# Causal attention stage: rows of maxima sent from ScalarE's queue, q and k loaded in six pairs over a group

## The reference

```
x = x + attn_a(layernorm(x))   # causal softmax attention, 16 heads of 16
x = x + ffn(layernorm(x))      # FP4 quantised SwiGLU, 256 -> 704 -> 256
x = x + attn_b(layernorm(x))   # rotary, local window of 128 and every 64th key
x = x + ffn(layernorm(x))
```

```
scores = einsum('bhqd,bhkd->bhqk', Q, K) / sqrt(16)
attn = softmax(scores + causal)      # causal: -inf above the diagonal
O = einsum('bhqk,bhkd->bhqd', attn, V)
```

## Time and profile before

| | us |
|---|---|
| median of 3 runs | 3343.1 |
| lowest, highest | 3340.86, 3345.84 |
| the profiled execution's own time | 3338.47 |
| its span in the trace | 3336.7 |
| span of the attention stage's matmuls, first turn to last turn | 292.3 to 1062.8 |

### The profile page before, as it was taken

One profiled execution on the slowest core, in us unless ns is written; L12 is line 12 of the kernel. 1 busy time (PEld: TensorE's weight loads), 2 busy tenths in 40 slices (PEclk: granted clock), 3 DMA queues, 4 the chain that ended last, 5 costly groups with the idle time before them and its releaser, 6 DMA issues. The chain is left out here.

```text
span 3336.7 us, 92235 instructions
## 1 busy us (share of the span) xinstructions
PE 3098.7 (93%) x34732; PEld 2145.9 (64%) x34828; DVE 2606.8 (78%) x5407; ACT 1746.1 (52%) x3395; POOL 1092.9 (33%) x1631
## 2 busy tenths in 40 slices
PE   3997999999999799999979969999999969999999
PEld 2654777777776477777755535565555537777776
DVE  6547999999997699999959955655655649999997
ACT  3653887788788333333326635555555533333333
POOL 2542121121122222222216654454454432222222
PEclk8996999999999899999989979999999979999999
DMA  3764434434432222222226664445445322222221
GB/s 112 229 218 99 106 90 103 103 90 107 99 89 66 84 85 86 85 86 85 82 70 205 198 161 112 103 110 115 102 108 112 82 72 81 85 85 86 87 87 51
DMA packets 390672, 351.79 MB, mean 105 GB/s; under 512 B 111814, under 2 KB 331846, under 8 KB 390214
## 3 DMA queue, kind: packets, MB, share of 16 engines
q1 hardware_dynamic: 390342, 347.10, 38.6%
HBM read 210.12 MB, written 135.27 MB: 104 GB/s over the span
## 5 line engine op out<-in xcount | busy, mean ns | idle before, releaser
L852 DVE TENSOR_REDUCE aA_nmax<-bank 128x1 f32<-128x512 f32 (+3 forms) x1216 | 714.6, 653 | 69.9 <-PE bank L911 63.6
L895 ACT ACTIVATE aA_prob<-bank 128x512 f32<-128x512 f32 (+1 forms) x1216 | 616.8, 581 | 208.1 <-PE bank L911 202.9
L911 PE MATMUL bank<-aA_ks,aA_qs 96*32 96x512 bf16 (+13 forms) x6144 | 513.0, 321 | 27.0 <-POOL aA_vq L829 24.2
L1279 DVE TENSOR_REDUCE aB_nmax<-bank 128x2 f32<-128x512 f32 (+1 forms) x512 | 324.0, 657 | 212.9 <-remote 120.4
L911 PE MATMUL bank<-aA_qs,aA_ks 99*32 99x512 bf16 (+11 forms) x6144 | 470.2, 314 | 3.5 <-ACT aA_prob L895 1.8
L836 POOL TENSOR_SCALAR_AFFINE_SELECT aA_prob<-aA_prob 128x512 f32<-128x512 f32 x256 | 160.9, 634 | 663.6 <-ACT aA_prob L895 663.6
L911 PE MATMUL bank<-aA_prob,aA_vq 128*32 128x512 f32 (+3 forms) x3072 | 355.9, 490 | 1.4 <-POOL aA_prob L836 0.9
L1342 ACT ACTIVATE aB_prob<-bank 128x512 f32<-128x512 f32 (+1 forms) x512 | 278.2, 572 | 107.9 <-PE bank L1373 103.5
L911 PEld LDWEIGHTS bank<-aA_ks,aA_qs 96*32 96x32 bf16 x6144 | 247.2, 96 | 131.7 <-DVE aA_nmax L852 44.6
L1373 PE MATMUL bank<-aB_ks,aB_qs 96*128 96x256 bf16 (+3 forms) x2048 | 244.7, 258 | 38.8 <-DMA aB_own<-own_d 28.6
L911 PEld LDWEIGHTS bank<-aA_qs,aA_ks 99*32 99x32 bf16 x6144 | 224.8, 96 | 57.1 <-ACT aA_prob L895 19.3
(11 more groups left out here) (240 smaller groups left out, 6497.4 us busy)
## 6 DMA issues: line engine op xcount, KB each, us to landing
parts_A<-pA_part SPq DMA_DIRECT2D x96, 256.0 KB, 3.3
aA_qs<-parts_A SPq DMA_DIRECT2D x192, 128.0 KB, 3.9
aA_ks<-parts_A SPq DMA_DIRECT2D x192, 128.0 KB, 4.0
parts_B<-pB_part SPq DMA_DIRECT2D x96, 256.0 KB, 2.6
aB_qs<-parts_B SPq DMA_DIRECT2D x192, 128.0 KB, 3.9
aB_ks<-parts_B SPq DMA_DIRECT2D x192, 128.0 KB, 4.0
o_A<-aA_o_sb SPq DMA_DIRECT2D x32, 512.0 KB, 3.0
o_B<-aB_o_sb SPq DMA_DIRECT2D x32, 512.0 KB, 3.1
```

Source lines behind the costliest of these rows:

```text
L852: nc.vector.tensor_reduce(dst, src, AX.X, ALU.max, negate=True).then_inc(s["m_taken"], 1)
L895: nc.scalar.activation(dst, src, ACT.Exp, scale=SCALE).then_inc(s["e_taken"], 1)
L911: return nc.tensor.matmul(out, lhsT, rhs, start=start, stop=True, skip_group_check=True)
L1279: nc.vector.tensor_reduce(dst, src, AX.X, ALU.max, negate=True).then_inc(s["max_taken"], 1)
```

## The change

Three things change, in the first attention stage alone.

1. The three DMAs of the maxima's rows leave SyncE's list and enter ScalarE's (`send_rows`), behind the same wait on `rows_ready`. Their place is set by the planner, where they are a piece "rows" on "act" with a cost of 500 ns and a due time of -0.2; a pseudo-engine "dma" adds 3500 ns until they have landed.
2. SyncE waits before each of the six pairs of loads of q and k: pair r of group n+4 waits for pv unit r of group n+1. Before, all six waited once, for the last pv of group n. The load of v for group n+2 moves ahead of them. The first loads of group 3 no longer stand behind the rows of group 0.
3. The planner gets the new costs (5000 ns for q and k in place of 12000, with the new condition), and its order for TensorE, VectorE and ScalarE comes out different.

```diff
-        put("sp qk", "qk", 0, 12000, -2, ("pe", "pv", n - RING, N_PV - 1))
+        put("sp qk", "qk", 0, 5000, -2, ("pe", "pv", n - RING + 1, N_PV // 2))
...
-        put("sp rows", "rows", 0, 3500, 0, ("dve", "turn", n, 0))
+        put("act", "rows", 0, 500, -0.2, ("dve", "turn", n, 0))
+        put("dma", "land", 0, 3500, 0, ("act", "rows", n, 0))
...
-            put("pe", "exp", i, 0.42 * cols - (20 * len(heads) if q0 == 0 else 0) + 5, at, ("sp rows", "rows", n, 0), line="e")
+            put("pe", "exp", i, 0.42 * cols - (20 * len(heads) if q0 == 0 else 0) + 5, at, ("dma", "land", n, 0), line="e")
...
                     b, g = n // NG, n % NG
-                    if n >= RING:
-
-                        sp.wait_ge(s["pv_done"], (n - RING + 1) * N_PV)
                     for r in range(NP6):
+                        if n >= RING:
+
+                            sp.wait_ge(s["pv_done"], (n - RING + 1) * N_PV + r + 1)
                         sp.dma_start(qs[g][r:KROWS:NP6, :, :],
                                      parts_v[Q_PART[r], g, b]).then_inc(qk_loaded[g], 16)
...
-                def load_rows(n):
-
-                    g = n % NG
-                    sp.wait_ge(s["rows_ready"], n + 1)
-                    for j in range(3):
-                        sp.dma_start(qs[g][KROWS + j:KROWS + j + 1, :, :].rearrange("o h (k t) -> o (h k) t", t=P),
-                                     rows[g % 2][:, j, :]).then_inc(m_loaded[g % 2], 16)
...
-                load_rows(0)
                 load_qk(3)
                 for n in range(NQ):
-                    if n + 1 < NQ:
-                        load_rows(n + 1)
-                    else:
+                    if n == NQ - 1:
                         invert_sums()
                     store_o(n)
+                    if n + 2 < NQ:
+                        load_v(n + 2)
                     if n + RING < NQ:
                         load_qk(n + RING)
-                    if n + 2 < NQ:
-                        load_v(n + 2)
...
-                pieces = {"exp": exp_unit, "out": out}
+                def send_rows(n, _):
+
+                    g = n % NG
+                    act.wait_ge(s["rows_ready"], n + 1)
+                    for j in range(3):
+                        act.dma_start(qs[g][KROWS + j:KROWS + j + 1, :, :].rearrange("o h (k t) -> o (h k) t", t=P),
+                                      rows[g % 2][:, j, :]).then_inc(m_loaded[g % 2], 16)
+
+                pieces = {"exp": exp_unit, "out": out, "rows": send_rows}
                 for kind, n, i in DENSE_PLAN["act"]:
                     pieces[kind](n, i)
```

## The result

| | before | after |
|---|---|---|
| median of 8 runs | 3345.02 | 3361.87 |
| lowest, highest | 3340.86, 3353.91 | 3354.43, 3366.26 |
| the profiled execution's own time | 3338.47 | 3358.38 |
| its span | 3336.7 | 3356.6 |

The ratio is 1.0046, with a 95% interval of 1.0032 to 1.0059: slower by 16.8 us. The forecast was 3360, slower.

The account below looks back on a forecast made before the run. TensorE was taken to bound the stage, VectorE close behind; +1.0 new stop, -0.2 old stop, -0.2 order, -0.1 covered stops gave +0.5 to +0.6 us a group, times 31 +17, 3355.5, plus 4.6 to the median: 3360 us; range 3338 to 3387.

Parts of the forecast that it names:

- The bound and the stage: In the changed attention stage TensorE is the bound, busy 197.7 of 200 us; 24.55 us a group plus 0.3 stray stops.
- The hold on ScalarE: Between exp 30 and exp 31, three row-transfer starts hold ScalarE's sequencer 1.82 us, from 1.94 to 3.76 after the turn.
- The stop at exp 34: TensorE waits before exp 34 until ScalarE has taken exp 31 and freed its bank: 1.0 us a group.
- "Nothing gives it back": Behind the stop, nothing in the group recovers it, as TensorE's work is unchanged and it is the bound: 0.
- The order, and the old stop at exp 34: In each group, smoother alternation of max and exp units gains 0.2 us, and the old stop's 0.2 us goes.
- Part 2 at nothing: SyncE's spread q and k loads and earlier v load, hidden with 16 us of margin, were costed at nothing.
- Rival D: As forecast, but spread loads also delay TensorE's instruction fetches; stray stops double, +0.3 us a group, 3370 us; chance 0.04.
- What was not in the sum: For row-transfer starts on ScalarE, the sum took 1.82 us for three and no term for longer single starts.
- A: Whole ScalarE hold felt: starts wait for exp 30's end or cost 0.9 us each; +42 us, 3385 us; chance 0.11.
- B: No ScalarE hold felt, starts ending by 2.8 or activations starting meanwhile; order's gain remains: -12 us, 3331 us; chance 0.15.
- C: The stop before exp 34 is there but the order pays for it, +1.0 - 0.9: within 6.7 us of 3343; chance 0.13.

Follow-up runs that it names:

- e1: Changed kernel with its order and spread loads, but the three row transfers start on SyncE again, ahead of the output's store: 3326.67 us, ratio 0.9955 to before.
- e3: Changed kernel, but the three row parts lie on 96 partitions and go in one transfer on ScalarE's queue, same place: 3331.17 us, ratio 0.9965 to before.
- e4: Kernel before, old order, rows on SyncE; only the loads change: v moved ahead, q and k in six spaced pairs: 3329.95 us, ratio 0.9957.
- e5: Changed kernel with each of the three row transfers on ScalarE's queue cut in two, six starts, same bytes: 3480.63 us, ratio 1.0411 to before.
- e10: Kernel before with spaced pairs of q and k loads, and v loaded between the fifth and sixth pair: 3327.70 us, ratio 0.9965.
- e9: Kernel before with spaced pairs of q and k loads, and v still loaded behind them: 3330.89 us, ratio 0.9970.

## Why the prediction was right, and where it was not

**The bound and the stage**: right. The difference is all between the first and the last turn, and no row of after points elsewhere.

**The hold on ScalarE**: right, nearly to the number. Starts from 1.94 to 3.76 were forecast, 1.85 to 3.64 measured; 1.82 us for three, 1.79 measured; exp 31 at 3.86, and 3.74 measured where no start is stretched (median of all groups 4.06). The 0.1 that I added because VectorE has max 5 ahead of the turn did not come. The one estimate without a row, that a start costs on ScalarE what it costs on SyncE, held (0.61 and 0.59). The two rules read from the earlier trace rows held too: a busy datapath doesn't hold the sequencer (701.00, under the copy); a wait does (in 30 of 31 groups the first transfer starts 1.84 to 1.86 after the turn, though exp 30's scores are there before).

**The stop at exp 34**: the right place, a little large. Forecast 1.0 us; undisturbed 0.87 (1.11 against 0.24 in e1), the difference being the 0.1 just named. e3 shows that it is this hold and nothing else in the change: with 0.73 us of starts in the same place and order it is gone.

**"Nothing gives it back"**: wrong by 0.17 us a group. TensorE had small waits for banks behind the stop that the stop swallows. The argument was that TensorE's work per group is the same and it is the bound; but its beat held those waits too, and they are not work.

**The order, and the old stop at exp 34**: -0.4 forecast, -0.03 measured (e4 against e1). This is the term that was most wrong in size. I took 0.2 of the 1.1 us a group of weight loads' waits as gain, 6 us; the trace shows 17 us of these waits gone and 1 us gained. The runs don't part the two halves of the term.

**Part 2 at nothing**: wrong for the kernel without the hold, where it is worth 12 us (e4). The row was there: "issue" 5.8 us in 9 times, and 0.3 us a group between 24.55 and 24.85. I took these stops for a property of TensorE's own instruction supply, gave back only 0.1 a group for those that the new stop covers, and did not ask what was running when they fell. Rival D even had the loads acting on them, with the wrong sign: I thought that spreading would add to the stops, and it was the burst that went with them.

**What was not in the sum**: one start in 16 of 30 groups takes 0.9 to 1.6 us instead of 0.6, which adds 9.4 us to the stop, one for one. The earlier trace rows had the sign of it, a maximum of 1.93 us; on SyncE it had cost nobody anything, and I took the median.

**How the errors met**: forecast +0.5 to +0.6 a group, measured +0.63. Term by term: stop 0.87 for 1.0, given back 0.17 for 0, order and old stop 0.04 (periods 24.53 to 24.50) for 0.4, spaced loads 0.32 (24.85 to 24.53) for 0.1, stretched starts 0.31 for 0. 0.87 - 0.17 - 0.04 - 0.32 + 0.31 = 0.65. So 3360 against 3361.87 is better than the steps deserve: errors of 0.1 to 0.4 us a group cancelled. The range stated, 3338 to 3387, was wide: it held "no change" too.

**The rivals.** A (whole hold felt, 0.9 us per start or no overlap): falls, since starts begin under the copy and cost 0.61; the stretched starts are its grain of truth. B (no hold felt): falls for this kernel, and e3 shows its deciding point from the other side. I put it at starts that end by 2.8; e3's ends at about 2.6 and is not felt. The rule from the Trainium skill, "Advanced Engine Details and Errata", section "Sequencer and Instruction Queues", that others can be queued while such an instruction runs, the trace does not bear out for activations behind it: exp 31 starts 0.1 us after the last start has ended (0.38 us in a few groups), in after as in e5, though its scores were made long before. C (the order pays): falls, 0.03. D: falls with its sign. The rule of the Trainium skill, "DMA: Bandwidth & Descriptors", section "Issuing engines are not separate DMA queues", that other engines' queues save only the issuing time, agrees with the trace: e1 to after wins nothing anywhere and SyncE's 1.8 us had been free.

**The best of these kernels** is e1 at 0.9955, with e4 (0.9957), e3 and e10 (0.9965 both) and e9 (0.9970) not told apart from it: take the spaced loads, and either leave the rows on SyncE or send them in one transfer.

## What to carry to other kernels

Count a transfer's start as work of the engine that starts it (here 0.6 us for each part of the rows), put it on the engine with nothing due behind it, and merge transfers before moving them; then check which unit stands next behind it and who waits for its bank. When you cost an edit at nothing, look at the stray stops in the trace and ask what else ran when they fell; a burst of large loads can go with them, and the edit that spaces it be the gain. Waits of weight loads count only as far as matmuls stand still with them.

## What the runs showed of the hardware

- A start costs mainly by the instruction and little by its size: 0.61 us on ScalarE for 32 partitions as for 16, 0.73 for 96 in one (e5, after, e3). Its form matters too: the store of an output took 0.34 us on SyncE. Three in one saves 1.1 us of sequencer time a group.
- An activation behind a start waits for its end (703.25 to 703.35), but the starts themselves run under an activation in progress (701.00 under the copy from 700.79).
- In after 16 of 87 starts (groups 2 to 30) took 0.9 to 1.6 us. In the raw records all 16 overlap in time with a packet of an instruction queue, and 21 of the 71 others do. No run tested that link.
- TensorE's granted clock stayed at 1.00 with a stop of 1 us in 25 and fell to 0.91 over the same 200 us with stops of about 3 to 4 us (0.50 right behind one, 526.5 to 530). The longer stops lengthened a group by 3.8 us where they themselves grew by 2.1.
